# Convolution taps folded into projection weights on TensorE, and a normalisation moved to ScalarE

## What is computed

```python
zxbcdt = X @ W_in.T                       # X: 8 x 512 x 128, W_in: 644 x 128
z, xBC, dt = jnp.split(zxbcdt, [D_INNER, D_INNER + CONV_DIM], axis=-1)   # 256, 384, 4
dt = jax.nn.softplus(dt + dt_bias)
# depthwise causal convolution, 4 taps, over the 384 channels of xBC
xBC = jax.nn.silu(conv(xBC, conv_w) + conv_b)
x, Bm, Cm = jnp.split(xBC, [D_INNER, D_INNER + D_STATE], axis=-1)
...                                       # h = h * exp(dt A) + dt B x ; y = C h  (a scan over 512 steps)
y = ys + D * x
y = y * silu(z)
y = y * rsqrt(mean(y * y) + EPS) * norm_w
x1 = layernorm(X + (y @ W_out.T + X))     # no gain and no shift: (r - mean) / sqrt(var + eps)
```

## Time and profile before

| what | value |
|---|---|
| timed runs, median of 3 | 961.95 us (960.44 to 968.97) |
| profiled execution, device time | 956.43 us |
| its span | 954.7 us |
| PE / DVE / ACT / POOL busy over the span | 78% / 68% / 51% / 43% |
| mean granted clock of PE | 0.89 of 2.4 GHz |
| end of the Mamba layer (last issue of its stores) | about 267 us |

### The profile page before, as it was taken

The page is one execution under the profiler, slowest core; times in us unless marked ns, Lnnn a source line. Parts: engine busy times, 40 slices in busy tenths (PEclk is TensorE's granted clock), DMA queues, the critical chain, the costliest instruction groups (busy, mean ns, idle before and its releaser), DMA issues. The chain is left out here.

```text
span 954.7 us, 18446 instructions
## 1 busy us (share of the span) xinstructions
PE 745.3 (78%) x5462; PEld 508.2 (53%) x5462; DVE 648.4 (68%) x1592; ACT 491.0 (51%) x1006; POOL 408.9 (43%) x524
## 2 busy tenths in 40 slices
PE   5888878887647187998989888989878897999600
PEld 3566655665434153454545444545335897999600
DVE  4788889888526394777778767878543476557753
ACT  3555555655127003656565646565646364656634
POOL 1244233442330011243545544554515558776864
PEclk8998898989869556999999989999979999999955
DMA  1000110100039631123434433330134222325431
GB/s 45 20 26 18 39 39 26 36 18 28 23 109 288 170 110 65 59 73 93 125 105 124 117 69 103 90 98 26 38 88 123 63 62 72 95 61 150 124 113 44
DMA packets 98638, 75.76 MB, mean 79 GB/s; under 512 B 15687, under 2 KB 89779, under 8 KB 98542
## 3 DMA queue, kind: packets, MB, share of 16 engines
q1 hardware_dynamic: 92214, 60.35, 23.0%
q0 software_dynamic: 5248, 10.70, 3.4%
q10 hardware_dynamic: 1080, 3.54, 1.1%
HBM read 44.49 MB, written 25.25 MB: 73 GB/s over the span
## 5 line engine op out<-in xcount | busy, mean ns | idle before, releaser
L1627 ACT ACTIVATE pb<-psB 128x512 f32<-128x512 f32 (+1 forms) x352 | 192.0, 559 | 203.6 <-PE psB L2068 179.5
L1737 DVE TENSOR_REDUCE mx<-psB 128x1 f32<-128x384 f32 (+3 forms) x352 | 207.8, 635 | 72.2 <-PE psB L2048 71.7
L2046 PE MATMUL psB<-kx,qx 72*128 72x384 bf16 (+3 forms) x512 | 143.2, 331 | 27.5 <-DMA kx<-k_parts 22.5
L2068 PE MATMUL psB<-qx,kx 75*128 75x256 bf16 (+3 forms) x512 | 131.1, 312 | 23.3 <-DMA qx<-mparts 18.8
L1584 POOL TENSOR_SCALAR_AFFINE_SELECT pb<-pb 128x512 f32<-128x512 f32 x112 | 71.0, 639 | 149.9 <-ACT pb L1627 149.0
L2048 PE MATMUL psB<-hide,ident 128*128 128x128 bf16 x512 | 108.5, 237 | 0.0
L2087 PE MATMUL psB<-pb,vx 128*32 128x512 f32 (+3 forms) x1024 | 97.9, 456 | 0.2 <-POOL pb L1584 0.2
L2157 PE MATMUL psB<-hT_e,w1t 128*128 128x128 f32 x624 | 85.3, 281 | 15.5 <-issue 9.4
L2068 PEld LDWEIGHTS psB<-qx,kx 75*128 75x128 bf16 x512 | 46.1, 101 | 94.3 <-ACT pb L1627 54.7
L1553 POOL DMA_INDIRECT results<-y_e,hin x78 | 78.3, 1003 | 39.4 <-ACT y_e L1666 20.3
L2157 PEld LDWEIGHTS psB<-hT_e,w1t 128*128 128x128 f32 x624 | 77.4, 195 | 18.1 <-issue 17.0
(11 more groups left out here) (240 smaller groups left out, 1352.9 us busy)
## 6 DMA issues: line engine op xcount, KB each, us to landing
qx<-q_parts SPq DMA_DIRECT2D x84, 96.0 KB
kx<-k_parts SPq DMA_DIRECT2D x72, 96.0 KB
hin<-slots SPq DMA_DIRECT2D x78, 65.0 KB
ys<-results SPq DMA_DIRECT2D x16, 256.0 KB, 3.4
q_parts<-qpart SPq DMA_DIRECT2D x8, 384.0 KB
k_parts<-kpart SPq DMA_DIRECT2D x8, 384.0 KB
kx<-k_parts ACTq DMA_DIRECT2D x24, 96.0 KB
xin<-in_L_attn_X SPq DMA_DIRECT2D x8, 256.0 KB
```

Of the source, the lines that this page charges most:

```text
L1627: nc.scalar.activation(pb[step % PBUF][:, h0:h0 + heads, 0:width], src, ACT.Exp).then_inc(exp_ready, 2 if u == NEXP - 1 else 1)
L1737: nc.vector.tensor_reduce(mx[:, h0:h0 + heads, qt], ps[:, S_BANK + u % banks, 0:heads * width].rearrange("p (h n) -> p h n", n=width), AX. ...
L2046: nc.tensor.matmul(out, qx[q][0:QK_ROWS, h0 + j, qt * P:(qt + 1) * P], kx[q][0:QK_ROWS, h0 + j, 0:width], start=True, stop=False)
L2068: ins = nc.tensor.matmul(out, kx[q][0:MAX_ROWS, 4 * g + h0 + j, kt * P:(kt + 1) * P], qx[q][0:MAX_ROWS, 4 * g + h0 + j, kt * P:SEQ], start ...
```

## The change

The four taps are multiplied into the projection's weights in the head: DVE scales the 128x128 weight block of each channel chunk by each tap's column (`taps_w`, twelve instructions), PE transposes the twelve blocks, ACT copies them out (`tapsT`, three instructions). In every row, `conv` then issues four accumulating matmuls for a channel chunk, each with one tap's weights and x shifted by that tap, into one bank. ACT's `conv_copy` adds the bias and writes `acc`; `taps` on DVE is gone. `normalise` moves from DVE to ACT, in the form r * rstd2 + shift1, where DVE computes `shift1` = -mean * rstd2 in one instruction of 128x4. `steps_dt` no longer has taps ahead of it.

```diff
--- before.py
+++ after.py
...
@@ -361,18 +366,30 @@
         def _(act):
             act.wait_ge(w_in_sem, 16 * 6)
             nc.scalar.activation(a_neg[:, :], a_log[:, :], ACT.Exp).then_inc(setup_sb, 1)
+            act.wait_ge(taps_ps, 1)
+            for c in range(CH):
+                nc.scalar.activation(tapsT[:, c, :, :].rearrange("p k n -> p (k n)"), bank(3 + c), ACT.Copy).then_inc(setup_sb, 1)
 
             def xT_copy(row):
                 act.wait_ge(xT_ps, row(1, 1))
                 act.wait_ge(z_ps, row(1, 0))
                 nc.scalar.activation(xT[:, :], bank(6), ACT.Copy).then_inc(xT_sb, 1)
 
-            def newest_tap(row, c):
+            def conv_copy(row, c):
 
                 act.wait_ge(conv_ps, row(3, c + 1))
                 act.wait_ge(silu, row(3, 0))
-                nc.scalar.activation(acc[:, c, :], bank(6 + c % 2), ACT.Identity, bias=cb[:, c:c + 1],
-                                     scale=cw[:, c, TAPS - 1:TAPS]).then_inc(tap0, 1)
+                nc.scalar.activation(acc[:, c, :], bank(6 + c % 2), ACT.Identity, bias=cb[:, c:c + 1]).then_inc(conv_done, 1)
+
+            def normalise(row, it, p):
+                act.wait_ge(shift_ready, row(1, 1))
+                act.wait_ge(x1_used[p % 2], (it + p // 2) * 16)
+                if it * 2 + p >= 2:
+                    act.wait_ge(x1b_ready, it * 2 + p - 1)
+                for t in range(TILES):
+                    ins = nc.scalar.activation(x1[p % 2][:, t, :], r[:, t, :], ACT.Identity, bias=shift1[:, t:t + 1],
+                                               scale=rstd2[:, t:t + 1])
+                ins.then_inc(x1_ready, 1)
 
             def softplus_exp(row):
 
@@ -441,9 +458,9 @@
             start = Row(0, 0)
             xT_copy(start)
             for c in range(2):
-                newest_tap(start, c)
+                conv_copy(start, c)
             softplus_exp(start)
-            newest_tap(start, 2)
+            conv_copy(start, 2)
             softplus_ln(start)
             silus(0, 0)
 
@@ -459,32 +476,40 @@
                 b_copy(row)
                 if not last:
                     softplus_exp(next_row)
-                    newest_tap(next_row, 0)
+                    conv_copy(next_row, 0)
                 decays(row, 2)
+                if not first:
+                    normalise(before, it, p - 1)
                 if not last:
-                    newest_tap(next_row, 1)
+                    conv_copy(next_row, 1)
                     softplus_ln(next_row)
-                    newest_tap(next_row, 2)
+                    conv_copy(next_row, 2)
                 decays(row, 3)
                 if not last:
                     silus(it, p + 1)
                 squares(row)
             all_rows(act, body)
             yT_copy(Row(BATCH // 2 - 1, 1))
+            normalise(Row(BATCH // 2 - 1, 1), BATCH // 2 - 1, 1)
 
         @block.vector
         def _(dve):
 
+            dve.wait_ge(proj_loaded, 16 * 3)
+            dve.wait_ge(w_in_sem, 16 * 6)
+            for c in range(CH):
+                for k in range(TAPS):
+                    nc.vector.tensor_scalar(taps_w[:, c, k, :], win[:, DI // P + c, :], cw[:, c, k:k + 1], None,
+                                            ALU.mult).then_inc(taps_scaled, 1)
             dve.wait_ge(setup_ps, 1)
             nc.vector.tensor_copy(winT[:, :], bank(0, 2)[:, 0:PROJ]).then_inc(setup_sb, 1)
-            dve.wait_ge(w_in_sem, 16 * 6)
             for k in range(2):
                 nc.vector.tensor_scalar(woutT[:, k, :], bank(2)[:, k * P:(k + 1) * P], nw[:, k:k + 1], None,
                                         ALU.mult).then_inc(setup_sb, 1)
-            dve.wait_ge(setup_sb, 4)
+            dve.wait_ge(setup_sb, 4 + CH)
             nc.vector.tensor_scalar(a_neg[:, :], a_neg[:, :], -1.0, None, ALU.mult).then_inc(setup_sb, 1)
-            dve.wait_ge(setup_sb, 5)
-            front, scan, tail = Chain(dve, front_own, 13), Chain(dve, scan_own, 5), Chain(dve, tail_own, 4)
+            dve.wait_ge(setup_sb, 5 + CH)
+            front, scan, tail = Chain(dve, front_own, 7), Chain(dve, scan_own, 5), Chain(dve, tail_own, 4)
 
             def steps_u(row):
 
@@ -496,21 +521,6 @@
                 dve.wait_ge(u_ready, row(3, 1))
                 nc.vector.scalar_tensor_tensor(out=absu[:, :, :], in0=u[:, :, :], scalar=-1.0, in1=u[:, :, :],
                                                op0=ALU.mult, op1=ALU.max).then_inc(u_ready, 1)
-
-            def taps(row, c):
-
-                dve.wait_ge(tap0, row(3, c + 1))
-                for k in range(TAPS - 1):
-                    s = TAPS - 1 - k
-                    if k:
-                        front.wait()
-                    ins = nc.vector.scalar_tensor_tensor(out=acc[:, c, s:SEQ], in0=bank(6 + c % 2)[:, 0:SEQ - s],
-                                                         scalar=cw[:, c, k:k + 1], in1=acc[:, c, s:SEQ],
-                                                         op0=ALU.mult, op1=ALU.add)
-                    if k < TAPS - 2:
-                        front.add(ins)
-                    else:
-                        ins.then_inc(conv_done, 1)
 
             def steps_e(row):
 
@@ -638,23 +648,15 @@
                 ins.then_inc(var_ready, 1)
                 tail.end()
 
-            def normalise(row, it, p):
+            def shift(row):
                 dve.wait_ge(var_ready, row(1, 1))
                 dve.wait_ge(rstd2_ready, row(1, 1))
-                dve.wait_ge(x1_used[p % 2], (it + p // 2) * 16)
-                if it * 2 + p >= 2:
-                    dve.wait_ge(x1b_ready, it * 2 + p - 1)
-                for t in range(TILES):
-                    ins = nc.vector.tensor_scalar(x1[p % 2][:, t, :], r[:, t, :], mv[:, t, 0:1], rstd2[:, t:t + 1],
-                                                  ALU.subtract, ALU.mult)
-                ins.then_inc(x1_ready, 1)
+                nc.vector.scalar_tensor_tensor(out=shift1[:, :], in0=mv[:, :, 0], scalar=-1.0, in1=rstd2[:, :],
+                                               op0=ALU.mult, op1=ALU.mult).then_inc(shift_ready, 1)
 
             start = Row(0, 0)
             steps_u(start)
-            taps(start, 0)
             steps_e(start)
-            taps(start, 1)
-            taps(start, 2)
             steps_dt(start)
 
             def body(it, p, first, last):
@@ -670,22 +672,17 @@
                 if not last:
                     steps_e(next_row)
                 if not first:
-                    normalise(before, it, p - 1)
-                if not last:
-                    taps(next_row, 0)
+                    shift(before)
                 masked(row, 2)
-                if not last:
-                    taps(next_row, 1)
                 states(row)
                 masked(row, 3)
                 if not last:
-                    taps(next_row, 2)
                     steps_dt(next_row)
                 y_steps(row, p)
             all_rows(dve, body)
             end = Row(BATCH // 2 - 1, 1)
             residual(end)
-            normalise(end, BATCH // 2 - 1, 1)
+            shift(end)
 
         @block.tensor
         def _(pe):
@@ -697,6 +694,11 @@
             for k in range(2):
                 ins = nc.tensor.transpose(bank(2)[:, k * P:(k + 1) * P], wout[:, k * P:(k + 1) * P], ident[:, :])
             ins.then_inc(setup_ps, 1)
+            pe.wait_ge(taps_scaled, CH * TAPS)
+            for c in range(CH):
+                for k in range(TAPS):
+                    ins = nc.tensor.transpose(bank(3 + c)[:, k * P:(k + 1) * P], taps_w[:, c, k, :], ident[:, :])
+            ins.then_inc(taps_ps, 1)
 
             def turn_x(it, p):
                 row = Row(it, p)
@@ -712,8 +714,11 @@
                     pe.wait_ge(u_ready, row(3, 1))
                 if c == 2:
                     pe.wait_ge(conv_done, row(3, 1))
-                nc.tensor.matmul(bank(6 + c % 2), winT[:, DI + c * P:DI + (c + 1) * P], xT[:, :],
-                                 start=True, stop=True).then_inc(conv_ps, 1)
+                for k in reversed(range(TAPS)):
+                    s = TAPS - 1 - k
+                    ins = nc.tensor.matmul(bank(6 + c % 2)[:, s:SEQ], tapsT[:, c, k, :], xT[:, 0:SEQ - s],
+                                           start=(s == 0), stop=(k == 0))
+                ins.then_inc(conv_ps, 1)
 
             def project_dt(row):
                 pe.wait_ge(xT_sb, row(1, 1))
@@ -798,7 +803,7 @@
                 ins.then_inc(o_ps, 1)
 
             turn_x(0, 0)
-            pe.wait_ge(setup_sb, 5)
+            pe.wait_ge(setup_sb, 5 + CH)
             pe.wait_ge(consts, 8)
             start = Row(0, 0)
             project_dt(start)
```

More of the change, by code:

```diff
@@ L105, in mamba_layer @@
         winT = sb("winT", [P, PROJ])
+        taps_w = sb("taps_w", [P, CH, TAPS, D])
+        tapsT = sb("tapsT", [P, CH, TAPS, P])
         wout = sb("wout", [P, DI])
@@ L157, in mamba_layer @@
         rstd2 = sb("rstd2", [P, TILES])
```

(5 more changed lines are left out.)

## The result

| what | before | changed |
|---|---|---|
| median of the timed runs | 961.79 us (4 runs) | 1013.5 us (4 runs, 1006.29 to 1016.97) |
| ratio | | 1.0558, 95% interval 1.0504 to 1.0612 |
| profiled execution, device time | 956.43 us | 1006.29 us |
| start of the last out-projection of the Mamba layer | 256.67 us | 307.52 us |
| from there to the end of the span | 698.0 us | 697.1 us |

The change costs 5.6%. All of it lies in the layer that was changed: its last out-projection starts 50.85 us later, and the rest of the program takes as long as before, to within 1 us of these two profiles. The ratios leave out slow executions, those over 1.5% above the fastest of their kernel, but the profiles of fold_only (1022.84 us) and before_filler (970.81 us) further down are of such ones.

The account below looks back on a forecast made before the run. PE was taken to bound some 13 us of a row, DVE 8. Rows +31.2, head +11.4, tail +0.8 and clock +3 sum to +46.4 on the profiled 956.43: 1002.8, raised toward the median to 1006 us; range 994 to 1021.

Parts of the forecast that it names:

- Place of the bound: In a first-layer row, PE limits some 13 us and DVE 8; removed DVE work gains 3.35 us per full row.
- (b): Row stretch from third state's matmul to last L206 group: 4.49 us before, 3.63 taken, a gain of 0.86.
- (a): Row stretch from out-projection to third state's matmul, set by PE; a wait of 0.28 us there was to go.
- (d): Row stretch from y transposes to next out-projection, 3.08 us, set by ACT's squares and yT copy; no gain was claimed.
- (c): Row stretch from last L206 group to y transposes, set by DVE: 8.12 us was to become 5.91.
- Price on PE: Nine more f32 matmuls per row in the PE-bound part, 0.85 us each, cost 7.65 us.
- not slower: Rival: a chunk's accumulating matmuls stream on PE at 0.25 us each, giving 960 to 965 us; chance 0.04.
- rival of 1.0 us for each: Each extra matmul on PE costs 1.0 us instead of 0.85, giving 1014 to 1019 us; chance 0.07.
- Head: Weight scaling, transposes and copies, then row 0's projections, start the next x's transposes 11.4 us later than 26.05.
- rival of a cheaper setup: Full clock from the start and overlapped scalings take 4 to 8 us off, 995 to 1002; chance 0.06.
- The clock: PE's clock falls behind the hole before the last L206 group: two losses of 1.5 us, +3 in all.
- the clock falls in every row: Rival: low PE clock behind each row's shorter hole, seven long falls at 2.5 us, 1017 to 1022; chance 0.13.

Follow-up runs that it names:

- fold_only: Changed kernel with the normalisation put back on DVE; ratio to before 1.0455.
- before_filler: Kernel before with two unused f32 matmuls added in the 2.8 us PE hole ahead of the last L206 group; ratio to before 0.9999.
- norm_only: Kernel before with only the normalisation moved to ACT, shift on DVE, taps left on DVE; ratio to before 0.995.
- after_filler: Changed kernel with two unused f32 matmuls added in the 1.87 us PE hole ahead of the last L211 group; ratio to before 1.0339.
- one_tap: Changed kernel with only one of the four accumulating matmuls per channel chunk, so the convolution is left out; 942.6 us, ratio to before 0.9824.
- two_taps: Changed kernel with two of the four accumulating matmuls per channel chunk, half the convolution left out; 971.7 us, ratio to before 1.0125.
- early_taps: Kernel before with normalisation on ACT, third convolution projection ahead of the fourth L198 and its taps ahead of the state copies; ratio to before 1.0108.
- z_in_hole: early_taps with the next row's z projection moved into the hole before the last L206 group, three unused matmuls in its old place; ratio to before 0.9911.

## Why the prediction was right, point by point

- **Place of the bound.** Right. PE bound the part up to the third chunk, DVE the part behind the last group. norm_only shows the first: 0.90 us a row for 3.2 us of DVE, where 0.86 and 0.28 for the wait were worked out. (b) fell by the 0.86, (a) by 0.34 in the mean, and (d) was 0.22 longer. after_filler shows the second: (c) is 5.90 where 8.12 - 2.21 = 5.91 was worked out. DVE was idle for more than the third of the layer that was named as a sign: it is busy for 139.3 of the first 317.5 us.
- **Price on PE.** Right: 0.86 for L198 was the right row. Four matmuls take 3.57 us (117.65 to 121.22), a little above the 3.4 to 3.5 named as a sign. Against the single one of before (1.06, 127.63 to 128.69) that is 0.84 for each of the three added, against that of one_tap (1.00) it is 0.86: all nine of a row 7.5 to 7.7 us, 7.65 predicted. The lower bound of 0.25 and with it the rival "not slower" are out, and so is the rival of 1.0 us for each.
- **(b).** 3.55 measured, 3.63 taken: the copy of a chunk lost 0.09 us with its scale operand (687 beside 777 ns), which the prediction had taken as hidden under DVE's state steps. norm_only, whose copies keep the scale, stays at 3.63, so this copy seems to lie on the path; it was not tried alone.
- **Normalisation on ACT.** 482 ns each, hidden, as said; fold_only shows no price and no gain of the move that stands clear of its interval.
- **Head.** Mis-sized: 11.4 predicted, 35.53 - 26.05 = 9.5 measured. The scalings took 2.4 us instead of 3.4, since they follow one another faster than four in 1.12 us did. The dt projection took 0.89 us (16.23 to 17.12) instead of 1.72. That part looks like luck: it is 0.89 in the changed kernel's second profile too, but 1.70 in those of one_tap, two_taps and fold_only, whose heads are the same up to there. The rival of a cheaper setup was thus right in kind, but got 1.9 us instead of 4 to 8.
- **Tail.** 0.8 predicted; from the last out-projection to the issue of the last store it is 9.96 us instead of 9.20, so 0.76.
- **The clock.** This is the term that was too small. The prediction took two losses of 1.5 us, 3 in all, from two holes of 1.95 and 2.04 us that had full speed right behind them. Right behind was the wrong place to look: in row 0 of before the clock fell some two microseconds after the group had begun (43.42). The windows of that row in the kernel before (clock in the last column but two):

```profile
44.00:45.00 1.00, 1.00 (x8) 0.95 (x8) 0.93 (x3) 0.95 (x1) 0.00 (x0) 1.00 0.00 0
46.00:48.00 2.00, 2.00 (x6) 1.53 (x6) 1.83 (x7) 0.25 (x1) 0.71 (x1) 0.50 0.24 52
49.00:50.00 1.00, 0.63 (x6) 0.48 (x4) 0.96 (x2) 0.68 (x1) 0.33 (x1) 1.00 0.00 0
```

  In the changed kernel all eight rows fell in the first profile and seven of eight in the second, and (c) took 6.84 to 7.94 us instead of 5.91, in two rows of the first with 0.45 more until the out-projection. The two prices were right: a short fall cost 6.84 - 5.90 = 0.94 us (about 1 predicted), a long one 7.94 - 5.90 + 0.45 = 2.49 (2.5 predicted). Wrong was how often: two losses were taken, eight came, two of them long. Over rows 1 to 6 the row is 35.28 instead of the 33.8 worked out at full speed: 6 x 1.5 = 9 us, and the last row, said to cost nothing, 24.89 instead of 23.59 (1.3). The rival "the clock falls in every row", which had a chance of 0.13, is what happened, at 1.5 us a row in the mean instead of its 2.5.
- **Sum.** At full clock the prediction had +43.4. Against it the head is 1.9 less, row 0 0.7 more (29.38 became 35.44 from its x transposes to the out-projection), rows 1 to 6 8.2 more (34.0 instead of 25.8), the last row 1.3 more: +51.7, and to the issue of the last store it is 317.48 - 265.87 = 51.6. The stages behind took 1.7 us less, so +49.9 in the profiled executions beside the +46.4 of the text. By medians the change cost 51.7 us; the forecast of 1006 was short of 1013.5 by 7.5. Of this 3.5 are the sum (49.9 beside 46.4) and 4.0 the step from profile to median: the changed kernel's median lies 7.2 above its own profiled execution, where 3.2 had been allowed for. That the sum came within 3.5 us is partly luck, since the rows took 10.2 us more than at full clock where 3 had been taken, and the missing 7.2 were offset by the head (1.9) and by the stages behind (1.7); and the time lies in the stated range because the range had been drawn out to the clock's rival.

## What to carry to other kernels

An operation that moves from one engine to another is worth nothing, or its full time, by where it stands between the waits of a row: nine taps and a normalisation of 9.9 us on DVE bought some 3.4 us at full clock, while the nine matmuls in their place cost all of their 7.65. Price a group of matmuls by the start-to-start time of the nearest one of the same shape and type. When another engine's work is shortened, look at what it had been hiding on PE, the low clock behind a hole above all. Filling the hole was worth 1.55 us a row in the changed kernel (35.28 to 33.73) and 2.03 in early_taps (29.56 to 27.53), and nothing in the kernel before, where DVE set the time behind it.

## What the runs showed of the hardware that I had not expected

- A hole of 1.87 us in PE's work, with dense work before it, was followed by the 1.2 GHz level in 15 of 16 rows of the changed kernel. It is not certain: in two_taps and one_tap, with the same hole and shorter rows, the clock stayed at 1.00 up to the y transposes in five of 16. With the hole filled to some 0.2 us the seven rows of after_filler that had the filler kept 1.00. In z_in_hole, with holes of 0.66, 0.73, 0.52 and 0.67 us, no row but the last fell.
- ScalarE on 128x512 f32 from PSUM took 597 ns with no per-partition operand (L418 of the kernel before, an Exp), 687 with a bias (L382) and 777 with bias and scale (L374): about 90 ns for each.
- The unchanged part of the program took from 695 to 711 us in thirteen profiles. A stretch of 300 us in it had a mean granted clock of 0.99 where it was shortest and 0.93 where it was longest. This is as large as the effect of the better variants and may be why their intervals are wide; what sets it stays open. The stretches inside the first layer that no fall of the clock touches repeat to 0.01 us in most rows.
